# One feed-forward stage of a Flamingo kernel: the operations of a step in another order, with four slots for the picked rows

## The chip, the cores and the metric

The kernel runs on one core of a Trainium2 chip. A core has TensorE (PE in the profile; its weight loads are a row of their own, PEld), VectorE (DVE), ScalarE (ACT), GpSimd (POOL) and SyncE (SP, which here issues DMAs). Each engine works through its own instructions in the order in which they are written and is held only by semaphores. The metric is the device time of one execution in microseconds (us); less is better.

## The reference, cut to what matters

The program is eight residual blocks over x, 32 batches of 128 rows by 128 columns. The change is in the sixth, the controller feed-forward. A low-rank product gives 8 groups of 64 logits per row; in each group the first of the largest logits picks one hidden unit of 64, and only the picked units go through the second matrix.

```python
def _L2_ffn_ref(x, m1, m2, mb, w1, w2, b2):
    lr = xf @ m1
    mask_logits = jnp.einsum('bl,lxy->bxy', lr, m2) + mb
    quant_mask = jnp.argmax(mask_logits, axis=-1)
    ...
    w = w1p[j, quant_mask]
    mid = jnp.einsum('ai,aji->aj', xf, w)
    relu = jax.nn.relu(mid)
    v = w2p[j, quant_mask]
    res = jnp.einsum('ai,aij->aj', relu, v) + b2
...
x = x + jnp.tanh(g_ffn[2]) * _L2_ffn_ref(_layernorm(x, axis=-1), ...)
```

## The kernel before

The stage takes the 32 batches one after the other. x stays on chip. For one batch (128 rows on the partitions) the kernel computes all 512 hidden units and zeroes those that are not picked. The work of a batch, by engine, with the lines of the kernel before:

- ACT: normalises the rows (`xn`, L2031), copies the transposed rows out of PSUM (`xt`, L2039), copies the low-rank values (`low`, L2046), applies the relu to all hidden units (`full`, L2050), copies the transposed picked rows (`rt`, L2054).
- PE: transposes `xn` (L2117), multiplies by m1 (L2130, "low"), by m2 (L2113, "logits"), by w1 (L2127), transposes the picked rows in four pieces (L2135, "picked transposes"), multiplies them by w2 (L2123, "y").
- DVE, with the names used below: **top** (L2078, largest logit of each group, out of PSUM), **compare** (L2085, logit >= top, written to `pick`), then on GpSimd **count** (L2018, `pick` times a descending count, so that of equal logits the first has the largest value), then on DVE again **code** (L2074, the largest count of each group), **first** (L2081, count == code), **product** (L2091, that mask times the relu of the w1 row, written to `pick`), at last **update** (L2095, adds gate times y to x) and **statistics** (L2098, `bn_stats` of the new rows for the next block's layernorm).
- GpSimd also adds the bias row to x (L2014).

Top, compare, code, first and product each work on 128x512 numbers. `pick` has two slots, one per batch in turn.

The order is written out by hand: each engine has a function `step` that lists what it does in one step for different batches, and `pipeline4` calls it. In step b of the kernel before, DVE does code of batch b-1, top of b, first of b-1, compare of b, product of b-1, update of b-2 and statistics of b-2. `pipeline4` writes out steps -1 to 3, loops over steps 4 to 29, two to a turn of the loop, and writes out the last four. Semaphores (`ge_ready` from compare, `coded` from count, `picked_ready` from product, and so on) hold an engine until its operand is there, or until a buffer is free. Another stage of the same program, `attention_over_heads`, already runs four steps to a turn of its loop; it is `pipeline6` in the kernel before.

## Time and profile before

| | us |
|---|---|
| median of 3 runs (1623.01 to 1623.5) | 1623.44 |
| the profiled execution | 1622.37 |
| its span in the trace | 1620.6 |
| PE busy in the span | 1384.5 |
| DVE busy in the span | 1004.6 |
| POOL busy in the span | 769.8 |
| ACT busy in the span | 734.3 |

The profiled execution lasted 1.77 us longer than its span, and 1.07 us less than the median of the runs. The shares of the whole span mix eight blocks with different limits, so the stage that is changed has to be looked at by itself: it runs from about 816 to 965 us of the span.

### The profile page before, as it was taken

The page shows a single profiled execution, that of the slowest core. Times are in us where ns is not written, and L with a number is a line of the kernel's source. Part 1 is how long each engine was busy: PE and PEld are TensorE (multiplying, and loading weights), DVE is VectorE, ACT ScalarE, POOL GpSimd, SP SyncE. Part 2 cuts the span into 40 slices and gives each one's busy share as a digit, 9 for nine tenths or more (in the row PEclk, how much of TensorE's full clock was granted, in tenths as well). Part 3 has the DMA queues.
Part 4 walks back from the last instruction along what each step waited for, and adds up shares of the span by engine and source line. Part 5 has one row for each costly group of instructions (what it writes and reads, how often), then busy time and mean ns, then how long its engine had stood idle before and what let it go on. Part 6 is the DMA issues. An engine that isn't in the chain of part 4 may idle for free. (4 is left out here: it accounts for less than half of the span.)

```text
span 1620.6 us, 33970 instructions
## 1 busy us (share of the span) xinstructions
PE 1384.5 (85%) x10919; PEld 1114.7 (69%) x10919; DVE 1004.6 (62%) x2272; ACT 734.3 (45%) x1831; POOL 769.8 (47%) x989
## 2 busy tenths in 40 slices
PE   4998776989756786999978977999999999696996
PEld 3777556989756564777745546887788777486984
DVE  4887862413388486999868873555656755363555
ACT  3677453323366544666544443445554454221121
POOL 2554582345272363555635433544444677206445
PEclk9999897999955796999989998999999999798999
DMA  6500033759210000000000000000000000375942
GB/s 187 191 1 2 13 106 90 214 167 270 83 43 10 1 1 1 1 0 0 2 0 0 0 1 0 1 0 0 1 2 1 11 21 15 107 228 171 300 144 85
DMA packets 96490, 100.08 MB, mean 62 GB/s; under 512 B 12149, under 2 KB 69677, under 8 KB 95726
## 3 DMA queue, kind: packets, MB, share of 16 engines
q1 hardware_dynamic: 62322, 69.60, 14.2%
q0 software_dynamic: 8192, 16.79, 3.5%
q10 hardware_dynamic: 25852, 12.09, 2.7%
q8 instruction: 70, 1.15, 0.3%
q14 instruction: 54, 0.44, 0.1%
HBM read 72.23 MB, written 26.21 MB: 61 GB/s over the span
## 5 line engine op out<-in xcount | busy, mean ns | idle before, releaser
L2229 POOL TENSOR_TENSOR exp_scores_xattn<-exp_scores_xattn,softmax_recip_xattn 128x1640 f32<-128x1640 f32 x32 | 93.5, 2922 | 162.6 <-DVE softmax_recip_xattn L2402 162.6
L1469 PE MATMUL psum<-sorted_transposed_ffn,tile_weights_up_ffn 128*128 128x128 f32 x1280 | 164.8, 283 | 4.2 <-DVE sorted_transposed_ffn L1357 4.1
L1469 PEld LDWEIGHTS psum<-sorted_transposed_ffn,tile_weights_up_ffn 128*128 128x128 f32 x1280 | 154.2, 197 | 11.5 <-DVE sorted_transposed_ffn L1357 11.3
L1243 POOL DMA_INDIRECT gathered_rows_ffn<-sorted_y,slot_ffn x96 | 90.7, 945 | 105.2 <-DMA sorted_y<-expert_rows_ffn 46.8
L798 POOL TENSOR_TENSOR exp_scores<-exp_scores,softmax_recip 128x308 f32<-128x308 f32 x128 | 97.5, 784 | 78.9 <-DVE softmax_sum L892 78.9
L1479 PE MATMUL psum<-expert_weights_down_ffn,hidden_ffn 128*128 x960 | 123.8, 280 | 3.4 <-issue 2.8
L445 POOL TENSOR_TENSOR exp_scores<-exp_scores,softmax_recip 128x308 f32<-128x308 f32 x128 | 85.8, 702 | 80.1 <-DVE softmax_recip L614 79.9
L1232 POOL DMA_INDIRECT sorted_x<-xn_ffn,slot_ffn x64 | 61.3, 958 | 131.3 <-DVE slot_ffn L1117 112.3
L1479 PEld LDWEIGHTS psum<-expert_weights_down_ffn,hidden_ffn 128*128 128x128 f32 x960 | 115.8, 195 | 5.5 <-issue 5.5
L2278 ACT ACTIVATE exp_scores_xattn<-psum,scaled_negated_max_xattn 128x205 f32<-128x205 f32 x256 | 106.6, 451 | 0.0
L2469 PE MATMUL psum<-kv_transposed_xattn,queries_xattn 128*128 128x205 f32 x512 | 97.8, 346 | 3.4 <-DVE queries_xattn L2407 3.4
L640 PE MATMUL psum<-identity,exp_scores 128*77 128x128 f32 x512 | 81.4, 287 | 20.9 <-POOL exp_scores L445 13.8
L1272 ACT ACTIVATE hidden_ffn<-psum 128x512 f32<-128x512 f32 x80 | 47.7, 597 | 110.9 <-PE psum L1469 110.9
L2256 ACT COPY kv_transposed_xattn<-psum 128x205 f32<-128x205 f32 x32 | 10.6, 332 | 191.5 <-PE psum L2482 191.5
L2469 PEld LDWEIGHTS psum<-kv_transposed_xattn,queries_xattn 128*128 128x128 f32 x512 | 90.8, 196 | 4.0 <-DVE queries_xattn L2407 3.9
L2018 POOL TENSOR_TENSOR pick_ffn<-pick_ffn,descending_count 128x512 f32<-128x512 f32 x32 | 52.4, 1637 | 73.7 <-DVE pick_ffn L2085 73.7
L640 PEld LDWEIGHTS psum<-identity,exp_scores 128*77 128x77 f32 x512 | 62.6, 155 | 30.7 <-issue 22.7
L932 PE MATMUL psum<-identity,exp_scores 128*77 128x128 f32 x512 | 80.3, 281 | 3.1 <-POOL exp_scores L798 1.1
L2349 DVE TENSOR_REDUCE negated_max_xattn<-psum 128x4 f32<-128x820 f32 x64 | 64.7, 1010 | 25.4 <-PE psum L2469 25.0
L1278 ACT ACTIVATE silu_ffn<-psum 128x512 f32<-128x512 f32 x40 | 23.9, 597 | 123.3 <-PE psum L1469 120.7
L1357 DVE COPY sorted_transposed_ffn<-psum 128x256 f32<-128x256 f32 x80 | 33.7, 422 | 73.6 <-PE psum L1447 73.5
L1387 DVE COPY expert_rows_ffn<-psum 128x256 f32<-128x256 f32 x80 | 33.9, 424 | 70.8 <-PE psum L1479 67.1
(391 smaller groups left out, 3671.2 us busy)
## 6 DMA issues: line engine op xcount, KB each, us to landing
tile_weights_up_ffn<-in_L_ffn_packed_dram SPq DMA_DIRECT2D x160, 256.0 KB, 3.2
sorted_rows_ffn<-sorted_x SPq DMA_DIRECT2D x80, 128.0 KB, 3.1
sorted_y<-expert_rows_ffn ACTq DMA_DIRECT2D x80, 128.0 KB
sorted_x<-zeros SPq DMA_DIRECT2D x4, 1280.0 KB, 13.2
x_residual<-in_x_dram SPq DMA_DIRECT2D x4, 512.0 KB, 11.3
expert_weights_down_ffn<-in_L_ffn_packed_dram SPq DMA_DIRECT2D x8, 256.0 KB, 15.1
sorted_x<-xn_ffn,slot_ffn POOLq DMA_INDIRECT x128, 2.3
gathered_rows_ffn<-sorted_y,slot_ffn POOLq DMA_INDIRECT x128, 2.8
```

Of the source, the lines that this page charges most:

```text
L445: nc.gpsimd.tensor_tensor(e[:, par, heads, :], e[:, par, heads, :], rec.to_broadcast([S, HG, KC]), ALU.mult).then_inc(s["probs_ready"], 1)
L640: last = nc.tensor.transpose(m.psum[0:KC, 4 + g % 2, h * S:(h + 1) * S], e[:, nxt, g * HG + h, :], m.ident[:, :])
L798: nc.gpsimd.tensor_tensor(ev, ev, recip[:, ring % 2, :].unsqueeze(1).to_broadcast([S, HG, KC]), ALU.mult).then_inc(s["probs_ready"], 1)
L932: last = nc.tensor.transpose(m.psum[0:KC, 4 + g % 2, h * S:(h + 1) * S], e[:, (ring - 2) % RING, g * HG + h, :], m.ident[:, :])
L1232: nc.gpsimd.indirect_dma_start(m.sorted_x[half][:, :], bass.IndirectOffsetOnAxis(slot[:, half, k, b:b + 1], 0), xn[:, half * HBATCH + b, : ...
L1243: nc.gpsimd.indirect_dma_start(yg[:, n % 4, k, :], None, m.sorted_y[half][:, :], bass.IndirectOffsetOnAxis(slot[:, half, k, b:b + 1], 0)). ...
L1469: mm = nc.tensor.matmul(m.psum[:, 2 * (n % 2) + half, to:to + SUB], w[:, n % DEPTH, u, at:at + 128], xst[:, n % 2, u * SUB:(u + 1) * SUB], ...
L1479: mm = nc.tensor.matmul(m.psum[:, 4 + n % 2, u * D:(u + 1) * D], hid[:, n % 2, c, u * 128:(u + 1) * 128], columns(n, u, c * D), start=(c = ...
L2229: nc.gpsimd.tensor_tensor(ev, ev, recip[:, par, :].unsqueeze(2).to_broadcast([S, H3, KV]), ALU.mult).then_inc(s["probs_ready"], 1)
L2278: ins = nc.scalar.activation(e[:, par, h, :], m.psum[:, h // HB, (h % HB) * KV:(h % HB + 1) * KV], ACT.Exp, scale=SCALE, bias=shift_bias[: ...
L2349: nc.vector.tensor_reduce(negmax[:, par, heads].rearrange("p (n h) -> p n h", h=HB), sv, AX.X, ALU.max, negate=True).then_inc(s["negmax_re ...
L2469: mm = nc.tensor.matmul(m.psum[:, h // HB, (h % HB) * KV:(h % HB + 1) * KV], q[:, par, h, :], kvt[:, par, :], start=True, stop=True)
```

## The change

The stage gets `pipeline_fours`, which is `pipeline6` of the attention stage under a new name and with the first and the last step as arguments; `has(b, lag)` says for a written-out step whether the batch b - lag exists. The attention stage's own order stays as it was. In the controller feed-forward

- the steps run from -3 to 34 (before: -1 to 33), steps 4 to 27 in a loop of four steps to a turn;
- `pick` has four slots in place of two;
- on DVE a step is now: compare of batch b, update of b-3, statistics of b-4, top of b+1, then code, first and product of b-1 in a row. From compare to product of one batch there are eight operations on DVE in place of five;
- on ACT the copy of the picked transposes stands ahead of the copy of `xt`, and the relu is the first of a step;
- on PE a step is: w1 of b+1, picked transposes of b-2, transpose of b+3, logits of b+2, y of b-2, low of b+3;
- on GpSimd count stands ahead of the bias, which runs three batches ahead.

What is computed is the same, with the same instructions on the same shapes. The core of the diff, with removed lines left out (they are in the functions above):

```diff
@@ -737,14 +737,19 @@
-def pipeline6(eng, step, n=B):
-    for b in range(-2, 4):
+def has(b, lag):
+    return not isinstance(b, int) or 0 <= b - lag < B
+def pipeline_fours(eng, step, first, end, n=B):
+    for b in range(first, 4):
         step(b, b % 4)
     with eng.Fori(0, (n - 8) // 4) as i:
         for u in range(4):
             step(i * 4 + 4 + u, u)
-    for b in range(n - 4, n + 3):
+    for b in range(n - 4, end):
         step(b, b % 4)
...
@@ -1987,6 +1988,7 @@
     gate = m.gate[:, 6:7]
     HID = MX * MY
     CH = HID // 128
+    RING = 4
     with ExitStack() as ctx:
         def sb(name, shape, dtype=F32):
             return ctx.enter_context(nc.sbuf_tensor(f"{name}_ffn2", shape, dtype))
@@ -1998,7 +2000,7 @@
         full = sb("all_hidden", [S, 2, HID])
         top = sb("top_logit", [S, MX])
         code = sb("pick_code", [S, MX])
-        pick = sb("pick", [S, 2, MX, MY])
+        pick = sb("pick", [S, RING, MX, MY])
         rt = sb("picked_transposed", [128, CH * S])
         with nc.Block() as block:
             @block.gpsimd
@@ -2008,53 +2010,52 @@
                 pool.wait_ge(s["ones_ready"], 1)
                 pool.wait_ge(s["row_ready"], 1)
...
+                def step(b, ring):
+                    if has(b, 0):
                         wait(pool, s["ge_ready"], b + 1)
...
+                        pv = pick[:, ring, :, :]
                         nc.gpsimd.tensor_tensor(pv, pv, m.down[:, 0:MY].unsqueeze(1).to_broadcast([S, MX, MY]),
                                                 ALU.mult).then_inc(s["coded"], 1)
-                pipeline4(pool, step)
+                    if has(b, -3):
+                        wait(pool, s["xn_ready"], b + 4)
+                        nc.gpsimd.tensor_tensor(m.x[:, b + 3, :], m.x[:, b + 3, :], row_b2[:, :], ALU.add).then_inc(s["bias_added"], 1)
+                pipeline_fours(pool, step, -3, B + 3)
             @block.scalar
             def _(act):
                 act.wait_ge(s["var_ready"], 1)
                 nc.scalar.activation(m.sd[:, :], m.var[:, :], ACT.Sqrt, bias=m.eps[:, 0:1]).then_inc(s["sd_ready"], 1)
                 act.wait_ge(s["shift_ready"], 1)
                 def normalise(b, slot):
                     nc.scalar.activation(xn[:, slot, :], m.x[:, b, :], ACT.Identity, scale=m.rstd[:, bass.ds(b, 1)],
                                          bias=m.shift[:, bass.ds(b, 1)]).then_inc(s["xn_ready"], 1)
...
+                def step(b, ring):
+                    par, nxt = ring % 2, 1 - ring % 2
+                    if has(b, 0):
                         wait(act, s["full_in_psum"], b + 1)
                         wait(act, s["picked_ready"], b - 1)
                         nc.scalar.activation(full[:, par, :], m.psum[:, 3 + par, :], ACT.Relu).then_inc(s["full_ready"], 1)
...
+                    if has(b, -2):
+                        wait(act, s["low_in_psum"], b + 3)
+                        wait(act, s["logits_in_psum"], b + 1)
+                        nc.scalar.copy(low[0:ML, par, :], m.psum[0:ML, 0, S:2 * S]).then_inc(s["low_ready"], 1)
+                    if has(b, 2):
+                        wait(act, s["rt_in_psum"], b - 1)
+                        wait(act, s["y_done"], b - 2)
                         nc.scalar.copy(rt[:, :], m.psum[:, 5, :]).then_inc(s["rt_ready"], 1)
+                    if has(b, -3):
+                        wait(act, s["xt_in_psum"], b + 4)
+                        wait(act, s["full_in_psum"], b + 2)
+                        nc.scalar.copy(xt[:, nxt, :], m.psum[:, 0, 0:S]).then_inc(s["xt_ready"], 1)
+                    if has(b, -4):
+                        wait(act, s["xt_in_psum"], b + 3)
+                        normalise(b + 4, par)
                 normalise(0, 0)
-                pipeline4(act, step)
+                pipeline_fours(act, step, -3, B + 3)
                 preload(nc, m, ACT.Sqrt)
             @block.vector
@@ -2065,78 +2066,83 @@
                 nc.vector.tensor_scalar(row_b2[:, :], row_b2[:, :], gate, None, ALU.mult).then_inc(s["row_ready"], 1)
                 wide = [S, MX, MY]
...
+                def statistics(b):
+                    wait(dve, s["x_done"], b + 1)
+                    nc.vector.bn_stats(m.moments[:, b, :], m.x[:, b, :])
+                def logits_of(slot):
+                    return m.psum[:, 1 + slot, :].rearrange("p (x y) -> p x y", y=MY)
+                def step(b, ring):
+                    par, nxt = ring % 2, 1 - ring % 2
+                    last = pick[:, (ring - 1) % RING, :, :]
+                    if has(b, 0):
+                        wait(dve, s["top_ready"], b + 1)
+                        wait(dve, s["rt_in_psum"], b - 3)
+                        nc.vector.tensor_tensor(pick[:, ring, :, :], logits_of(par), top[:, :].unsqueeze(2).to_broadcast(wide),
+                                                ALU.is_ge).then_inc(s["ge_ready"], 1)
+                    if has(b, 3):
+                        wait(dve, s["y_done"], b - 2)
+                        wait(dve, s["bias_added"], b - 2)
+                        nc.vector.scalar_tensor_tensor(m.x[:, b - 3, :], m.psum[:, 6, 0:D], gate, m.x[:, b - 3, :],
+                                                       ALU.mult, ALU.add).then_inc(s["x_done"], 1)
+                    if has(b, 4):
+                        statistics(b - 4)
+                    if has(b, -1):
+                        wait(dve, s["logits_in_psum"], b + 2)
+                        wait(dve, s["ge_ready"], b + 1)
+                        nc.vector.tensor_reduce(top[:, :], logits_of(nxt), AX.X, ALU.max).then_inc(s["top_ready"], 1)
+                    if has(b, 1):
                         wait(dve, s["coded"], b)
...
+                        wait(dve, s["first_ready"], b - 1)
+                        nc.vector.tensor_reduce(code[:, :], last, AX.X, ALU.max).then_inc(s["code_ready"], 1)
                         wait(dve, s["code_ready"], b)
...
+                        nc.vector.tensor_tensor(last, last, code[:, :].unsqueeze(2).to_broadcast(wide), ALU.is_equal).then_inc(s["first_ready"], 1)
                         wait(dve, s["first_ready"], b)
                         wait(dve, s["full_ready"], b)
...
-                pipeline4(dve, step)
+                        picked = last.rearrange("p x y -> p (x y)")
+                        nc.vector.tensor_tensor(picked, picked, full[:, nxt, :], ALU.mult).then_inc(s["picked_ready"], 1)
+                pipeline_fours(dve, step, -3, B + 3)
+                statistics(B - 1)
             @block.tensor
             def _(pe):
                 pe.wait_ge(m.later_loaded, m.later_count)
                 pe.wait_ge(s["ones_ready"], 1)
...
+                def step(b, ring):
+                    par, nxt = ring % 2, 1 - ring % 2
+                    if has(b, -1):
+                        wait(pe, s["xt_ready"], b + 2)
+                        wait(pe, s["full_ready"], b)
+                        nc.tensor.matmul(m.psum[:, 3 + nxt, :], xt[:, nxt, :], w1[:, :], start=True, stop=True).then_inc(s["full_in_psum"], 1)
+                    if has(b, 2):
+                        wait(pe, s["picked_ready"], b - 1)
+                        wait(pe, s["rt_ready"], b - 2)
+                        for c in range(CH):
+                            mm = nc.tensor.transpose(m.psum[:, 5, c * S:(c + 1) * S],
+                                                     pick[:, (ring - 2) % RING, :, :].rearrange("p x y -> p (x y)")[:, c * 128:(c + 1) * 128], m.ident[:, :])
+                        mm.then_inc(s["rt_in_psum"], 1)
+                    if has(b, -3):
+                        wait(pe, s["xn_ready"], b + 4)
+                        wait(pe, s["low_ready"], b + 3)
+                        nc.tensor.transpose(m.psum[:, 0, 0:S], xn[:, nxt, :], m.ident[:, :]).then_inc(s["xt_in_psum"], 1)
+                    if has(b, -2):
+                        wait(pe, s["low_ready"], b + 3)
+                        wait(pe, s["ge_ready"], b + 1)
                         nc.tensor.matmul(m.psum[:, 1 + par, :], low[:, par, :], m2[:, :], start=True, stop=True).then_inc(s["logits_in_psum"], 1)
...
+                    if has(b, 2):
                         wait(pe, s["rt_ready"], b - 1)
                         wait(pe, s["x_done"], b - 2)
                         for c in range(CH):
                             mm = nc.tensor.matmul(m.psum[:, 6, 0:D], rt[:, c * S:(c + 1) * S], w2[:, c, :], start=(c == 0), stop=(c == CH - 1))
                         mm.then_inc(s["y_done"], 1)
...
+                    if has(b, -3):
+                        wait(pe, s["xt_ready"], b + 4)
                         nc.tensor.matmul(m.psum[0:ML, 0, S:2 * S], m1[:, :], xt[:, nxt, :], start=True, stop=True).then_inc(s["low_in_psum"], 1)
...
-                pipeline4(pe, step)
+                pipeline_fours(pe, step, -3, B + 3)
 def latent_attention(nc, m, sem, r, clear):
```

**DVE, one step inside the loop, before.** `pick_ffn` is the slot of picked rows, `top_logit_ffn` the largest logits, `pick_code_ffn` the code, `all_hidden_ffn` the relu of the w1 row.

```order
L2074 TENSOR_REDUCE pick_code_ffn<-pick_ffn 128x8
L54 REGISTER_ALU
L2078 TENSOR_REDUCE top_logit_ffn<-psum 128x8
L2081 TENSOR_TENSOR pick_ffn<-pick_ffn,pick_code_ffn 128x512
L2085 TENSOR_TENSOR pick_ffn<-psum,top_logit_ffn 128x512
L2091 TENSOR_TENSOR pick_ffn<-pick_ffn,all_hidden_ffn 128x512
L2095 ISA
L2095 SCALAR_TENSOR_TENSOR x_residual<-psum,tanh_gates,x_residual 128x128
L2098 ISA
L2098 BN_STATS x_moments<-x_residual 128x6
```

**DVE, one step inside the loop, now.**

```order
L2082 TENSOR_TENSOR pick_ffn<-psum,top_logit_ffn 128x512
L2087 ISA
L2087 SCALAR_TENSOR_TENSOR x_residual<-psum,tanh_gates,x_residual 128x128
L2071 ISA
L2071 BN_STATS x_moments<-x_residual 128x6
L54 REGISTER_ALU
L2094 TENSOR_REDUCE top_logit_ffn<-psum 128x8
L2098 TENSOR_REDUCE pick_code_ffn<-pick_ffn 128x8
L2100 TENSOR_TENSOR pick_ffn<-pick_ffn,pick_code_ffn 128x512
L2104 TENSOR_TENSOR pick_ffn<-pick_ffn,all_hidden_ffn 128x512
```

Before, the code of a batch came three instructions behind its compare (product, update, statistics lie between), and code, first and product had one other instruction between each two. Now a batch's code comes a whole step behind its compare, and code, first and product follow one another directly; statistics no longer follows the update of its own batch.

**PE, one step inside the loop, before.** `L_w` stands for w1 and w2, `L_m_and_mb` for m2 with its bias, `L_m` for m1.

```order
L2113 MATMUL psum<-L_m_and_mb,low_rank_ffn 128x512
L54 REGISTER_ALU
L2117 MATMUL psum<-identity,xn_ffn 128x128
L2123 MATMUL psum<-L_w,picked_transposed_ffn 128x128 x4
L2127 MATMUL psum<-L_w,xt_ffn 128x512
L2130 MATMUL psum<-xt_ffn,L_m 64x128
L2135 MATMUL psum<-identity,pick_ffn 128x128 x4
```

**PE, one step inside the loop, now.**

```order
L2119 MATMUL psum<-L_w,xt_ffn 128x512
L2124 MATMUL psum<-identity,pick_ffn 128x128 x4
L54 REGISTER_ALU
L2130 MATMUL psum<-identity,xn_ffn 128x128
L2134 MATMUL psum<-L_m_and_mb,low_rank_ffn 128x512
L2139 MATMUL psum<-L_w,picked_transposed_ffn 128x128 x4
L2143 MATMUL psum<-xt_ffn,L_m 64x128
```

The picked transposes (L2135, now L2124) stood last in a step, right ahead of the next step's logits; now the w1 product stands ahead of them. They are also of batch b-2 in place of b-1.

## Rows read from the trace of the kernel before

**Rows 1.** Busy time by stretch: PE, PEld, DVE, ACT, POOL, then granted clock, DMA.

```profile
823.50:965.00 141.50, 124.45 (x603) 71.38 (x602) 116.75 (x225) 63.30 (x156) 64.81 (x62) 0.97 0.00 0
827.00:830.40 3.40, 3.40 (x7) 0.87 (x5) 2.49 (x4) 0.66 (x2) 0.53 (x1) 0.50 0.00 0
958.00:964.60 6.60, 3.63 (x24) 2.77 (x24) 3.86 (x10) 1.27 (x3) 1.21 (x1) 1.00 0.01 1
```

**Rows 2.** Timeline of DVE: start, length, engine, line, operation, tiles [idle before].

```profile
884.46 0.68 DVE L2085 TENSOR_TENSOR pick_ffn<-psum,top_logit_ffn 128x512 f32<-128x512 f32 x1
...
885.66 0.34 DVE L2095 SCALAR_TENSOR_TENSOR x_residual<-psum,tanh_gates,x_residual 128x128 f32 x1
886.14 0.29 DVE L2098 BATCH_NORM_STATS2 x_moments<-x_residual  x1
886.91 0.69 DVE L2074 TENSOR_REDUCE pick_code_ffn<-pick_ffn 128x8 f32<-128x512 f32 x1 [0.47 <-POOL pick_ffn L2018]
...
888.71 0.68 DVE L2085 TENSOR_TENSOR pick_ffn<-psum,top_logit_ffn 128x512 f32<-128x512 f32 x1
```

**Rows 3.** Timeline of POOL in the fill, and in the same step as rows 2.

```profile
824.44 1.26 POOL L2018 TENSOR_TENSOR pick_ffn<-pick_ffn,descending_count 128x512 f32<-128x512 f32 x1 [3.77 <-DVE pick_ffn L2085]
...
885.22 1.65 POOL L2018 TENSOR_TENSOR pick_ffn<-pick_ffn,descending_count 128x512 f32<-128x512 f32 x1 [2.20 <-DVE pick_ffn L2085]
```

**Rows 4.** Timeline of PE in the loop.

```profile
884.06 1.02 PE L2127 MATMUL psum<-L_w,xt_ffn 128*128 128x512 f32 x2
885.01 0.43 PE L2130 MATMUL psum<-xt_ffn,L_m 128*64 128x128 f32 x2
885.80 0.66 PE L2135 MATMUL psum<-identity,pick_ffn 128*128 128x128 f32 x4 [0.35 <-DVE pick_ffn L2091]
886.29 1.02 PE L2113 MATMUL psum<-L_m_and_mb,low_rank_ffn 65*128 65x512 f32 x2
887.15 0.27 PE L2117 MATMUL psum<-identity,xn_ffn 128*128 128x128 f32 x1
887.26 1.05 PE L2123 MATMUL psum<-L_w,picked_transposed_ffn 128*128 128x128 f32 x8
888.15 1.02 PE L2127 MATMUL psum<-L_w,xt_ffn 128*128 128x512 f32 x2
```

**Rows 5.** Timeline of DVE, the last steps of the stage.

```profile
959.24 0.69 DVE L2074 TENSOR_REDUCE pick_code_ffn<-pick_ffn 128x8 f32<-128x512 f32 x1 [0.57 <-POOL pick_ffn L2018]
959.96 0.69 DVE L2081 TENSOR_TENSOR pick_ffn<-pick_ffn,pick_code_ffn 128x512 f32<-128x512 f32 x1
960.68 0.69 DVE L2091 TENSOR_TENSOR pick_ffn<-pick_ffn,all_hidden_ffn 128x512 f32<-128x512 f32 x1
...
964.35 0.29 DVE L2098 BATCH_NORM_STATS2 x_moments<-x_residual 128x6 f32<-128x128 f32 x1
```

**Rows 6.** Timeline of DVE in the attention stage's loop, four steps to a turn.

```profile
660.05 0.34 DVE L916 SCALAR_TENSOR_TENSOR x_residual<-psum,tanh_gates,x_residual 128x128 f32 x1
660.35 0.80 DVE L886 TENSOR_TENSOR head_sums<-exp_scores 128x616 f32<-128x616 f32 x1
...
666.28 0.80 DVE L886 TENSOR_TENSOR head_sums<-exp_scores 128x616 f32<-128x616 f32 x1 [0.25 <-issue]
```

**Rows 7.** Timeline of PE, then of DVE, in the fill.

```profile
820.84 2.07 PE L2113 MATMUL psum<-L_m_and_mb,low_rank_ffn 65*128 65x512 f32 x2 [0.35 <-ACT low_rank_ffn L2046]
822.70 0.42 PE L2117 MATMUL psum<-identity,xn_ffn 128*128 128x128 f32 x1
822.92 1.91 PE L2127 MATMUL psum<-L_w,xt_ffn 128*128 128x512 f32 x2
824.76 0.69 PE L2130 MATMUL psum<-xt_ffn,L_m 128*64 128x128 f32 x2
...
829.71 0.68 DVE L2091 TENSOR_TENSOR pick_ffn<-pick_ffn,all_hidden_ffn 128x512 f32<-128x512 f32 x1
```

**Rows 8.** The product's 32 lengths: shortest, median, longest, first and last start.

```profile
L2091 DVE TENSOR_TENSOR pick_ffn<-pick_ffn,all_hidden_ffn x32: 678/680/693, 829.7 to 960.7; 128x512 f32<-128x512 f32 x32
```

More of the change, by code:

```diff
@@ L765, in attention_over_heads @@
     RING = 4
-    def has(b, lag):
-        return not isinstance(b, int) or 0 <= b - lag < B
     with ExitStack() as ctx:
@@ L810, in step @@
                         scale(ring, range(1, NG))
-                pipeline6(pool, step)
+                pipeline_fours(pool, step, -2, B + 3)
             @block.scalar
@@ L991, in step @@
                         transposes(b, ring, 3)
-                pipeline6(pe, step)
+                pipeline_fours(pe, step, -2, B + 3)
 class Routing:
@@ L2032, in normalise @@
                                          bias=m.shift[:, bass.ds(b, 1)]).then_inc(s["xn_ready"], 1)
-                def step(b, par, front, middle, back, tail):
-                    nxt = 1 - par
-                    if front:
-                        wait(act, s["xt_in_psum"], b + 2)
-                        wait(act, s["full_in_psum"], b)
-                        nc.scalar.copy(xt[:, nxt, :], m.psum[:, 0, 0:S]).then_inc(s["xt_ready"], 1)
-                    if front and not (isinstance(b, int) and b + 2 >= B):
-                        wait(act, s["xt_in_psum"], b + 1)
-                        normalise(b + 2, par)
-                    if front:
-                        wait(act, s["low_in_psum"], b + 2)
-                        wait(act, s["logits_in_psum"], b)
-                        nc.scalar.copy(low[0:ML, nxt, :], m.psum[0:ML, 0, S:2 * S]).then_inc(s["low_ready"], 1)
-                    if middle:
+                def step(b, ring):
+                    par, nxt = ring % 2, 1 - ring % 2
+                    if has(b, 0):
                         wait(act, s["full_in_psum"], b + 1)
@@ L2066, in _ @@
                 wide = [S, MX, MY]
-                def step(b, par, front, middle, back, tail):
-                    nxt = 1 - par
-                    pv = pick[:, nxt, :, :]
-                    if back:
-                        wait(dve, s["coded"], b)
-                        nc.vector.tensor_reduce(code[:, :], pv, AX.X, ALU.max).then_inc(s["code_ready"], 1)
-                    if middle:
-                        wait(dve, s["logits_in_psum"], b + 1)
-                        logits = m.psum[:, 1 + par, :].rearrange("p (x y) -> p x y", y=MY)
-                        nc.vector.tensor_reduce(top[:, :], logits, AX.X, ALU.max).then_inc(s["top_ready"], 1)
-                    if back:
-                        wait(dve, s["code_ready"], b)
-                        nc.vector.tensor_tensor(pv, pv, code[:, :].unsqueeze(2).to_broadcast(wide), ALU.is_equal).then_inc(s["first_ready"], 1)
-                    if middle:
-                        wait(dve, s["top_ready"], b + 1)
-                        wait(dve, s["rt_in_psum"], b - 1)
-                        nc.vector.tensor_tensor(pick[:, par, :, :], logits, top[:, :].unsqueeze(2).to_broadcast(wide),
-                                                ALU.is_ge).then_inc(s["ge_ready"], 1)
-                    if back:
@@ L2105, in _ @@
                 pe.wait_ge(s["ones_ready"], 1)
-                def step(b, par, front, middle, back, tail):
-                    nxt = 1 - par
-                    if middle:
-                        wait(pe, s["low_ready"], b + 1)
-                        wait(pe, s["ge_ready"], b - 1)
-                        nc.tensor.matmul(m.psum[:, 1 + par, :], low[:, par, :], m2[:, :], start=True, stop=True).then_inc(s["logits_in_psum"], 1)
-                    if front:
-                        wait(pe, s["xn_ready"], b + 2)
-                        wait(pe, s["low_ready"], b + 1)
-                        nc.tensor.transpose(m.psum[:, 0, 0:S], xn[:, nxt, :], m.ident[:, :]).then_inc(s["xt_in_psum"], 1)
-                    if tail:
+                def step(b, ring):
[18 more added lines that the diff above has]
+                        wait(pe, s["ge_ready"], b + 1)
+                        nc.tensor.matmul(m.psum[:, 1 + par, :], low[:, par, :], m2[:, :], start=True, stop=True).then_inc(s["logits_in_psum"], 1)
+                    if has(b, 2):
                         wait(pe, s["rt_ready"], b - 1)
```

34 lines of the change are left out of this document (2 added, 32 removed).

## The prediction, made before the changed kernel was run

> **What bounds the stage now.** I read the busy time by stretch first. In the 141.5 us of the stage PE is busy for 124.5 us and DVE for 116.8 us [rows 1]: neither is full, and no transfer runs, so something goes round between engines. The timeline of DVE over one step shows what. From one compare to the next it is 888.71 - 884.46 = 4.25 us, and in each step DVE stands idle once, for 0.47 us ahead of code, until POOL's count has ended [rows 2]. The timeline of POOL closes the ring: compare starts at 884.46, count at 885.22 (0.76 later), code at 886.91 (1.69 later), and behind code stand top, first and the next compare, three starts in 1.80 us [rows 2, 3]. 0.76 + 1.69 + 1.80 = 4.25: the whole period. The reader is to see that compare of batch b waits behind first of b-1, which waits for count of b-1. DVE's own work would take 0.47 us less. PE follows: it waits 0.35 us in the shown step for the product [rows 4].
>
> **What the change does to this ring.** Count of batch b starts when compare has ended, 0.76 us into DVE's step, and is done at 2.45; code of b is now in the next step, and nothing of DVE's own step waits for count. The slack is some 3 us (code starts about 1.7 us into the next step, 3.7 + 1.7 - 2.45). So the 0.47 us goes. The four slots carry this: a slot is written again four batches later, so compare need not wait for the picked transposes of its own slot (they end within two steps). More slots add no instruction; with only two, compare of b would have to wait for the transposes of b-2, which PE does in the same step.
>
> **What a DVE step costs now.** The sum of the start-to-start times in the new order:
>
> - compare to update 0.60, the pitch of independent wide operations (1.80 for three) [rows 2].
> - update to statistics 0.30: statistics is now of the batch before and waits for nothing in front of it. An update followed by an operation independent of it is 0.30 long [rows 6]; in the stage's loop, dependent, it was 0.48 [rows 2].
> - statistics to top 0.20: it is 0.29 long [rows 2], and DVE's operations start about 0.08 ahead of their predecessor's end (0.68 long, 0.60 apart) [rows 2].
> - top to code 0.60.
> - code to first, first to product 0.72 each. These pairs are now neighbours, each reading what the one in front wrote. The last batch of the stage before shows exactly this pair: 959.24, 959.96, 960.68 [rows 5]. That is 0.12 more than independent neighbours, twice a step.
> - product to the next compare 0.60.
>
> Sum 3.74 us, against 4.25: the stall and the statistics' dependence go, two dependent pairs come. Below, the pairs cost 0.60 each: 3.50. Above, update to statistics stays at 0.48 and statistics holds top to its end and a little more (0.33): 4.05. I take 3.74, because rows 5 are these very instructions and rows 6 come from a loop of this very form. Such a loop also costs something at each return: 0.25 us of idle that nothing releases, and the start that is no longer early, 0.28 together [rows 6], once per four steps, six times.
>
> The Trainium skill (VectorE: DVE Perf Modes, section "The DRAIN you can't avoid") says that a chain of operations with a semaphore after each takes no longer than one without. By that rule first and product would cost no more than any neighbour, the sum would be 3.50, and the stage some 7.4 us shorter than by mine. Rows 5 against rows 2 differ by 0.12 for the same shapes, so I go by the rows.
>
> **What is late next.** PE's own step, from starts in the loop: w1 0.95, low at most its length 0.43, picked transposes 0.49, logits 0.86, transpose 0.11, y 0.89 [rows 4]: 3.73 at most, 3.52 if low costs as much as two of y's eight pieces (0.22). So PE is nearly as full as DVE and close behind it, but not ahead. Its waits: the relu of b now stands first on ACT and waits for product of b-2 (two slots of `full`); the copy of low is queued behind it, and transpose and logits wait for that copy. From the product's end this is relu 0.59, copy 0.26 and the two hand-overs, about 0.9 us, while PE is in the picked transposes for 0.5 to 0.6 of it. PE then trails DVE by some 0.3 us a step, but its delay doesn't come back: top of b+1 uses logits that PE made a step earlier, update uses y of a step earlier. ACT's copy of the picked transposes ahead of `xt` comes in time for y, which has logits (0.86) in front of it. GpSimd's bias, three batches ahead, has the rest of count's step.
>
> **The sum.** From the first product to the last it was 960.68 - 829.71 = 130.97 us [rows 5, 7], 31 steps. Now: 27 full steps of 3.74 are 100.98; step 2 has neither update nor statistics and its top stands right behind compare (0.72 + 0.60 + 0.72 + 0.72 + 0.60 = 3.36); step 3 lacks statistics (3.54); step 31 has no top (3.14); step 32 neither top nor compare (2.54). With six loop returns of 0.28 this is 115.2: **15.7 us less**.
>
> Against this stands the fill. The first product now stands behind top of batch 2, so PE must have made three logits before it. At half clock (0.50 until 830.4) [rows 1] logits take 1.86, a transpose 0.22, w1 1.84, and low between 0.44 (twice 0.22) and its length of 0.69 [rows 7]. A round is 4.4 to 4.6. The first logits started at 820.84; they now have a transpose in front of them, 821.06, so the third start at 829.8 to 830.3 and, with the clock rising on the way, end at about 831.4. Top, code, first: 0.1 + 0.60 + 0.72 + 0.72 put the first product at 833.5, **3.8 us later** than before. Bounds 3.4 and 4.4 (clock rising a microsecond earlier or later). The tail behind the last product is the same chain as before, with one more statistics at the end: 0.2 us.
>
> Net 15.7 - 3.8 - 0.2 = 11.7. I round to 11.5. The profiled execution was 1622.37, so 1610.9; the median of the runs lies 1.07 above it, at 1623.44. **Forecast for the median: 1612.0 us.** The later stages start earlier and are otherwise as they were; no transfer ran in the stage that could now come too late [rows 1].
>
> **The rivals.**
>
> 1. *A step costs more than 3.74.* The order adds semaphore and register work to DVE's short operations, or PE at 3.73 plus its own loop return is the bound. At 4.05 over 27 steps 8.4 us of the gain go: 1620.3. For it: PE's sum is within 0.01 of DVE's at its upper bound. Against it: rows 6. Chance 0.20 for 1615.5 to 1620.2.
> 2. *Dependent neighbours cost nothing* (the skill's rule above). DVE's step is 3.50 and PE's 3.52 is the bound: 27 steps of 0.22 and the short ones give some 7 us more, 1605. Against it: rows 5. Chance 0.07, under 1609.
> 3. *Nothing gained: POOL and DVE slow each other.* Count took 1.26 us with DVE idle and 1.65 beside DVE [rows 3]. If in the new overlap DVE's operations were stretched by the same 0.39 a step, 31 steps lose 12.1 us: 1624. Against it: product ran beside count in every step and its length hardly moved, 678 to 693 ns [rows 8]. The Trainium skill (GPSIMD Engine Reference, section "Key points") has GpSimd contend with VectorE instructions that have two SBUF inputs; here the rows show the loss on POOL's side, where there is slack. Chance 0.08 for no change.
> 4. *Slower: PE's clock stays at its lower level.* In the fill it is 0.50, the lower level [rows 1]. A PE step there costs twice 3.52, or 3.3 us more than DVE's step. The gain of 11.5 is used up after 3.5 such steps, and 4.5 make the kernel measurably slower; a rise 35 us later (9 steps) gives 1642. For it: the fill is rearranged. Against it: with 0.50 until 830.4 the whole stretch still has 0.97, so the clock rose there and stayed, after a fill as nearly unbroken as the new one; and it was 1.00 in the stage's tail with PE busy for 3.63 of 6.60 us [rows 1]. Chance 0.05.
>
> **Numbers.** Forecast as it stands (1609 to 1615.5) 0.60. The range 1606 to 1619 takes in most of rivals 1 and 2, and leaves out about 0.2. A measurement of this kernel can tell about 0.2%, 3.2 us, from no change: under 1620.2 is faster, 0.60 + 0.20 + 0.07 = 0.87; same 0.08; slower 0.05.
>
> **What would show it.** Right: no idle ahead of code (L2098 in the new kernel) put down to count; compares 3.7 to 3.8 us apart, with one longer gap in four; first 0.72 behind code, and product 0.72 behind first; the first product near 833.5 and the last near 949. Wrong: idle on DVE ahead of top or update released by PE (rival 1), wide DVE operations above 0.69 (rival 3), or a granted clock under 1.00 past 840 us (rival 4).

## The result, and the profile after

| | before | changed |
|---|---|---|
| median of the runs, us | 1623.22 (4 runs, 1622.12 to 1623.5) | 1610.57 (4 runs, 1607.57 to 1612.35) |
| ratio to before | | 0.9927 (95%: 0.9913 to 0.9941) |
| span of the profiled execution, us | 1620.6 | 1605.8 |
| the stage in that span, us | 148.57 | 134.66 |

The kernel is faster by 0.73%, 11.9 us (9.6 to 14.1); the medians of the table alone lie 12.65 us apart, inside that range. The stage is taken here and below from the first operation of its layernorm (`x_mean_doubled` on DVE) to the same operation of the next block:

```profile
813.69 0.22 DVE L317 TENSOR_TENSOR x_mean_doubled<-x_moments 128x32 f32<-128x32 f32 x1 [0.55 <-PEq L790]
...
948.35 0.22 DVE L317 TENSOR_TENSOR x_mean_doubled<-x_moments 128x32 f32<-128x32 f32 x1 [0.31 <-PEq L2005]
```

Before, these two stood at 816.37 and 964.94. The stage gave 13.9 us of the 14.8 us between the two spans. What lies ahead of it was 2.7 us shorter in this execution and what lies behind it 1.8 us longer, with the same code: that much moves by itself from run to run, so small effects are read from the stage, and the smallest from the step, since PE's clock moves the stage's two ends too (shown with the experiments).

Busy time over 95 us of the steady steps (PE, PEld, DVE, ACT, POOL, then granted clock and DMA), to be held against [rows 1]:

```profile
840.00:935.00 95.00, 95.00 (x486) 60.07 (x485) 93.22 (x180) 48.90 (x125) 43.01 (x51) 1.00 0.00 0
```

PE has no idle time left and DVE 1.8 us in 95. One step of DVE, from compare to compare, which answers to [rows 2]:

```profile
879.58 0.68 DVE L2082 TENSOR_TENSOR pick_ffn<-psum,top_logit_ffn 128x512 f32<-128x512 f32 x1
880.18 0.34 DVE L2087 SCALAR_TENSOR_TENSOR x_residual<-psum,tanh_gates,x_residual 128x128 f32 x1
880.44 0.28 DVE L2071 BATCH_NORM_STATS2 x_moments<-x_residual  x1
880.64 0.67 DVE L2094 TENSOR_REDUCE top_logit_ffn<-psum 128x8 f32<-128x512 f32 x1
881.23 0.68 DVE L2098 TENSOR_REDUCE pick_code_ffn<-pick_ffn 128x8 f32<-128x512 f32 x1
881.94 0.69 DVE L2100 TENSOR_TENSOR pick_ffn<-pick_ffn,pick_code_ffn 128x512 f32<-128x512 f32 x1
882.66 0.69 DVE L2104 TENSOR_TENSOR pick_ffn<-pick_ffn,all_hidden_ffn 128x512 f32<-128x512 f32 x1
883.27 0.68 DVE L2082 TENSOR_TENSOR pick_ffn<-psum,top_logit_ffn 128x512 f32<-128x512 f32 x1
```

The wait ahead of code is gone and a step is 3.69 us. Code to first is 0.71 and first to product 0.72, where independent neighbours stand 0.59 to 0.61 apart. POOL in the same step, beside [rows 3]:

```profile
880.34 1.27 POOL L2017 TENSOR_TENSOR pick_ffn<-pick_ffn,descending_count 128x512 f32<-128x512 f32 x1 [2.02 <-DVE pick_ffn L2082]
881.57 0.46 POOL L2021 TENSOR_TENSOR x_residual<-x_residual,L_b_row 128x128 f32 x1
```

Count is 1.27 us long in place of 1.65. It ends at 881.61, the bias behind it at 882.03, and first starts at 881.94. One step of PE, beside [rows 4]:

```profile
877.36 0.60 PE L2124 MATMUL psum<-identity,pick_ffn 128*128 128x128 f32 x4
877.80 0.27 PE L2130 MATMUL psum<-identity,xn_ffn 128*128 128x128 f32 x1
877.91 1.02 PE L2134 MATMUL psum<-L_m_and_mb,low_rank_ffn 65*128 65x512 f32 x2
878.77 1.05 PE L2139 MATMUL psum<-L_w,picked_transposed_ffn 128*128 128x128 f32 x8
879.76 0.43 PE L2143 MATMUL psum<-xt_ffn,L_m 128*64 128x128 f32 x2
880.12 1.13 PE L2119 MATMUL psum<-L_w,xt_ffn 128*128 128x512 f32 x2
881.08 0.60 PE L2124 MATMUL psum<-identity,pick_ffn 128*128 128x128 f32 x4
```

PE takes 3.72 us in this step, 3.73 in the mean of the loop, and waits for nothing: the two engines are nearly even, with PE 0.03 to 0.04 us a step behind.

### The profile page after: what moved, and what is told of

It is laid out like the page before. It is cut to its first block and busy times, and to the rows that moved or that the text cites. A ratio compares the mean times of both kernels' runs of the same rounds, so it can differ in the third digit from the quotient of the medians.

```text
span 1605.8 us, 33990 instructions
## 1 busy us (share of the span) xinstructions
PE 1376.9 (86%) x10919; PEld 1113.0 (69%) x10919; DVE 1004.9 (63%) x2272; ACT 732.2 (46%) x1831; POOL 757.8 (47%) x989
## 5 line engine op out<-in xcount | busy, mean ns | idle before, releaser
L2524 PE MATMUL psum<-probs_t_context_xattn,kv_kept_xattn 77*128 77x512 f32 x128 | 68.0, 612 | 9.2 <-ACT probs_t_latents_xattn L2276 8.4
## 6 DMA issues: line engine op xcount, KB each, us to landing
x_residual<-in_x_dram SPq DMA_DIRECT2D x4, 512.0 KB, 10.9
```

The lines of the kernel that those rows point to most:

```text
L2524: nc.tensor.matmul(m.psum[:, 4 + half, :], kept[0:KC, nxt, 0, :], ptc[:, cols], start=True, stop=False)
```

## The experiments

All times are in us. The stage is that of one profiled execution. "Step" is the mean distance between DVE's compares from batch 8 to batch 24, from the timeline; PE's granted clock is 1.00 there in every kernel.

| kernel | median | before, same chip | ratio (95%) | stage | step |
|---|---|---|---|---|---|
| before | 1623.22 | | | 148.57 | 4.26 |
| changed | 1610.57 | 1623.22 | 0.9927 (0.9913 to 0.9941) | 134.66 | 3.70 |
| before_half_count | 1619.8 | 1622.14 | 0.9979 (0.9964 to 0.9993) | 145.58 | 4.18 |
| before_late_transposes | 1625.32 | 1622.66 | 1.0016 (1.0004 to 1.0029) | 151.01 | 4.25 |
| before_half_count_late_transposes | 1611.41 | 1622.66 | 0.995 (0.9933 to 0.9967) | 136.34 | 3.79 |
| after_two_slots | 1644.36 | 1622.14 | 1.0131 (1.0104 to 1.0158) | 169.31 | 4.76 |
| after_rt_copy_last | 1626.93 | 1622.14 | 1.0031 (1.0019 to 1.0044) | 151.30 | 4.35 |
| after_count_twice | 1639.68 | 1622.14 | 1.0098 (1.0073 to 1.0124) | 165.42 | 4.71 |
| after_interleaved | 1616.68 | 1622.66 | 0.9966 (0.9951 to 0.9981) | 140.13 | 3.89 |
| after_interleaved_clear_of_count | 1609.17 | 1622.66 | 0.9923 (0.9902 to 0.9944) | 133.05 | 3.73 |
| after_three_pieces | 1608.84 | 1620.88 | 0.9923 (0.9904 to 0.9942) | 134.36 | 3.69 |
| clear_of_count_three_pieces | 1602.28 | 1620.88 | 0.9886 (0.9862 to 0.9909) | 125.02 | 3.45 |
| clear_of_count_early_pe | 1607.82 | 1620.88 | 0.9911 (0.9895 to 0.9928) | 133.05 | 3.74 |

A stage also holds what PE's clock did at its two ends, and that is not the edits' doing alone. The changed kernel and after_three_pieces (below) have the same PE instructions in the fill, and their first transposes start at 816.33 and 816.40. These rows, one of each kernel, show the stretch in which the granted clock rises from 0.50 to 1.00 (last column but two):

```profile
828.00:829.00 1.00, 1.00 (x3) 0.10 (x2) 0.00 (x0) 0.97 (x3) 0.44 (x1) 0.84 0.00 0
```

```profile
824.00:826.00 2.00, 2.00 (x6) 0.63 (x5) 0.96 (x2) 0.76 (x3) 0.46 (x1) 0.81 0.00 0
```

So it rose 12.0 us after the first transpose in one and 8.4 in the other, and the first product came 17.36 and 15.67 us after the stage's start. In before it rose after 11.9 us; over all kernels, after 8.4 to 15.5. In the last 7 to 11 us of the stage the clock fell to 0.50 again in before_late_transposes, after_two_slots, after_count_twice, after_interleaved and after_three_pieces, and stayed at 1.00 in the others. Differences between stages of some 2 us are therefore not read by themselves; the step is.

### Was count's ring the bound of before?

The first kernel makes count shorter in the order of before.

```diff
-                        pv = pick[:, par, :, :]
-                        nc.gpsimd.tensor_tensor(pv, pv, m.down[:, 0:MY].unsqueeze(1).to_broadcast([S, MX, MY]),
+                        pv = pick[:, par, 0:MX // 2, :]
+                        nc.gpsimd.tensor_tensor(pv, pv, m.down[:, 0:MY].unsqueeze(1).to_broadcast([S, MX // 2, MY]),
```

Expected: 

> The order of before, with count on 4 of the 8 groups, about 0.85 us in place of 1.65 (leaves out half of the count). Theory (the ring compare, count, code, top, first sets before's step of 4.25 us): the ring falls to some 3.45 us, DVE's own 3.78 us or PE's 3.75 us takes over, so 0.45 us x 31 steps: 12 to 14 us less than before, as much as the whole change. Rival (PE's order makes the gain, POOL's wait is only where PE's limit shows): 0 to 2 us less.

The stage fell by 3.0 us, not by 12 to 14, and the step from 4.26 to 4.18. The theory of one ring, as the prediction had it, failed here. DVE's and PE's timelines of this kernel show what took over:

```profile
883.65 0.69 DVE L2074 TENSOR_REDUCE pick_code_ffn<-pick_ffn 128x8 f32<-128x512 f32 x1
884.64 0.69 DVE L2078 TENSOR_REDUCE top_logit_ffn<-psum 128x8 f32<-128x512 f32 x1 [0.30 <-PE psum L2113]
...
886.44 0.68 DVE L2091 TENSOR_TENSOR pick_ffn<-pick_ffn,all_hidden_ffn 128x512 f32<-128x512 f32 x1
...
887.18 0.66 PE L2135 MATMUL psum<-identity,pick_ffn 128*128 128x128 f32 x4 [0.35 <-DVE pick_ffn L2091]
887.75 1.12 PE L2113 MATMUL psum<-L_m_and_mb,low_rank_ffn 65*128 65x512 f32 x2
...
888.90 0.69 DVE L2078 TENSOR_REDUCE top_logit_ffn<-psum 128x8 f32<-128x512 f32 x1 [0.29 <-PE psum L2113]
```

Code no longer waits, but top does, for PE. From top to product it is 1.80, to the picked transposes 0.74, to the logits queued behind them 0.57, to the next top 1.15: 4.26 us (4.10 in the other step of the loop's turn). So before had a second ring, product, transposes, logits, top, just under the first. The next two kernels cut it by PE's order, with the full count and with half of it.

```diff
 PE, one step:
-  logits(b), transpose(b+1), y(b-2), w1(b), low(b+1), picked transposes(b-1)
+  logits(b), picked transposes(b-2), transpose(b+1), w1(b), low(b+1), y(b-2)
 ACT, one step:
-  xt(b+1), normalise(b+2), low(b+1), relu(b), rt(b-1)
+  rt(b-2), xt(b+1), normalise(b+2), low(b+1), relu(b)
```

Expected: 

> The order of before on DVE and POOL, full count; on PE the picked transposes of b-2 behind the logits of b, and y last, ACT's copy of them first. Theory of two rings (one over count, 4.25 us; one over product, picked transposes, logits, top, 4.1 to 4.25): this cuts only the second, the first stays: within 2 us of before. Rival (PE's order alone is the gain): 10 us under before.

Expected: 

> The same with count on 4 of 8 groups (leaves out half of the count). Theory of two rings: both are cut, DVE's own 3.78 us a step is left, 0.45 us x 31: 12 to 14 us under before, though each of the two edits alone gives 0 to 3. Rival (a third wait holds the step at 4.1 or more): under 4 us.

With the full count the step stayed at 4.25, and the stage got 2.4 us longer at its two ends, where the clock rose later (15.5 us after PE's first transpose) and fell to 0.50 before the end. With half of the count the step fell to 3.79 and the stage by 12.2 us, as expected; the whole kernel, by its ratio, by 8.1 (5.4 to 10.9). Alone the two edits take 0.08 and 0.01 us off the step, together 0.47: two rings of nearly the same length, and the gain comes only when both are cut. The changed kernel cuts both, since it makes the logits two batches ahead and transposes the picked rows two steps behind.

### The other parts of the change

Two slots in place of four:

```diff
-    RING = 4
+    RING = 2
...
-                        wait(dve, s["rt_in_psum"], b - 3)
+                        wait(dve, s["rt_in_psum"], b - 1)
```

Expected: 

> The changed kernel with two slots of picked rows in place of four, so that compare of b waits for the picked transposes of b-2, which PE does in the same step. Theory: DVE stands 0.6 to 0.75 us a step ahead of compare, steps of 4.35 to 4.45 us, 20 to 24 us above the changed kernel, some 10 us above before. Rival (the transposes end in time, slots are no part of the gain): the changed kernel's time.

The stage is 34.7 us longer than the changed kernel's, more than the expected 20 to 24. DVE's timeline:

```profile
885.09 0.69 DVE L2104 TENSOR_TENSOR pick_ffn<-pick_ffn,all_hidden_ffn 128x512 f32<-128x512 f32 x1
886.72 0.69 DVE L2082 TENSOR_TENSOR pick_ffn<-psum,top_logit_ffn 128x512 f32<-128x512 f32 x1 [0.94 <-PE psum L2124]
```

Compare waits 0.93 to 1.01 us a step in the loop (0.6 to 0.75 expected): the w1 product stands ahead of the transposes on PE and is still running when product ends. The slots are a condition of the gain.

ACT's copy of the picked transposes moved to the end of its step:

```diff
-                    if has(b, 2):
-                        wait(act, s["rt_in_psum"], b - 1)
-                        wait(act, s["y_done"], b - 2)
-                        nc.scalar.copy(rt[:, :], m.psum[:, 5, :]).then_inc(s["rt_ready"], 1)
                     if has(b, -3):
...
                         normalise(b + 4, par)
+                    if has(b, 2):
+                        wait(act, s["rt_in_psum"], b - 1)
+                        wait(act, s["y_done"], b - 2)
+                        nc.scalar.copy(rt[:, :], m.psum[:, 5, :]).then_inc(s["rt_ready"], 1)
```

Expected: 

> The changed kernel with ACT's copy of the picked transposes last in the step, behind the copy of xt and the normalise. Theory (PE is full at 3.73 us a step and y waits for this copy): the copy comes 0.6 to 0.7 us later, y too, and PE's step grows by as much: 16 to 20 us above the changed kernel, 4 to 8 us above before. Rival (DVE alone sets the step and PE's delay stays behind it): within 2 us of the changed kernel.

The stage grew by 16.6 us, as expected. PE waits for the copy, and DVE in turn for y:

```profile
883.74 1.16 PE L2139 MATMUL psum<-L_w,picked_transposed_ffn 128*128 128x128 f32 x8 [0.36 <-ACT picked_transposed_ffn L2055]
...
885.04 0.35 DVE L2087 SCALAR_TENSOR_TENSOR x_residual<-psum,tanh_gates,x_residual 128x128 f32 x1 [0.56 <-PE psum L2139]
```

So a delay on PE does come back to DVE, through update, as soon as PE's step is the longer one.

### Do POOL and DVE hold each other up?

Count done twice, on POOL:

```diff
...
+                        nc.gpsimd.tensor_tensor(pv, pv, down, ALU.mult).then_inc(s["counted_once"], 1)
+                        wait(pool, s["counted_once"], b + 1)
                         nc.gpsimd.tensor_tensor(pv, pv, down, ALU.mult).then_inc(s["coded"], 1)
```

Expected: 

> The changed kernel, with count done twice in a row on POOL (2.6 us or more in place of 1.27). Theory (count has some 3 us of slack now, DVE does not feel it): within 1.5 us of the changed kernel, 12 us under before. Rival (POOL and DVE slow each other where DVE reads two operands from SBUF): first and product get 0.2 us longer each in the steps, 10 to 12 us above the changed kernel, so about before's time.

My theory was wrong, and the rival too small: the stage is 30.8 us longer. DVE and POOL, from their timelines:

```profile
882.51 1.57 DVE L2102 TENSOR_TENSOR pick_ffn<-pick_ffn,pick_code_ffn 128x512 f32<-128x512 f32 x1
884.11 0.83 DVE L2106 TENSOR_TENSOR pick_ffn<-pick_ffn,all_hidden_ffn 128x512 f32<-128x512 f32 x1
...
882.26 1.27 POOL L2020 TENSOR_TENSOR pick_ffn<-pick_ffn,descending_count 128x512 f32<-128x512 f32 x1
883.48 0.91 POOL L2023 TENSOR_TENSOR x_residual<-x_residual,L_b_row 128x128 f32 x1
```

First (here L2102) is issued while the second count runs and is 1.57 us long, 0.88 more than alone. It ends at 884.08, 0.55 after that count; the bias, issued while first is there, is 0.91 in place of 0.46 and ends 0.31 after first; product is held by the rest of the bias (0.83). They do not share, they take turns. All of these read two tensors from SBUF. Statistics, top and code read one there at most; they start at 881.01, 881.21 and 881.80, beside the first count (880.91 to 882.18), and keep their lengths of 0.28, 0.67 and 0.67.

Whether this decides the order of DVE's step, the next two kernels show. Both put something between the dependent neighbours; the first places first beside count, the second behind it.

```diff
 DVE, one step:
-  changed:         compare(b), update(b-3), statistics(b-4), top(b+1), code(b-1), first(b-1), product(b-1)
+  interleaved:     compare(b), code(b-1), update(b-3), first(b-1), statistics(b-4), top(b+1), product(b-1)
+  clear of count:  compare(b), code(b-1), top(b+1), statistics(b-4), first(b-1), update(b-3), product(b-1)
```

Expected: 

> The changed kernel with DVE's step as compare, code, update, first, statistics, top, product, so that no operation reads what its neighbour wrote. Theory (a DVE instruction with two SBUF operands and one of POOL's wait for each other): first starts 1.5 us into the step, while count runs from 0.76 to 2.03, and is held for some 0.55 us; steps of about 4.0 us, 7 to 11 us above the changed kernel. Rival (no such wait, only the dependent pairs cost): DVE at 3.46 us a step, PE at 3.73 is the bound, 1 to 3 us under the changed kernel.

Expected: 

> The changed kernel with DVE's step as compare, code, top, statistics, first, update, product: no dependent neighbours, and first starts at 2.0 us, when count ends. Theory: DVE's step falls to some 3.5 us, PE at 3.73 us becomes the bound, and only the tail is shorter: 0 to 3 us under the changed kernel. Rival (DVE sets the step, PE follows it): 5 to 7 us under the changed kernel. If first is held by the bias too: 0 to 5 us above.

The first, beside count, costs 5.5 us of stage (7 to 11 expected) and 0.19 us a step: 0.43 of turn, less 0.24 for the two dependent pairs that are gone. The second saves 1.6 us of stage. Their rows of first, one after the other, the second with what stands in front of it on DVE and POOL's bias:

```profile
882.87 1.12 DVE L2095 TENSOR_TENSOR pick_ffn<-pick_ffn,pick_code_ffn 128x512 f32<-128x512 f32 x1
```

```profile
883.33 0.69 DVE L2091 TENSOR_REDUCE top_logit_ffn<-psum 128x8 f32<-128x512 f32 x1 [0.16 <-PE psum L2136]
883.89 0.46 POOL L2021 TENSOR_TENSOR x_residual<-x_residual,L_b_row 128x128 f32 x1
...
884.14 0.75 DVE L2096 TENSOR_TENSOR pick_ffn<-pick_ffn,pick_code_ffn 128x512 f32<-128x512 f32 x1
```

Beside count, first is 1.12 us (0.43 of turn, 0.55 expected). Behind count it still meets the bias, which POOL starts at once: 0.75 here, 0.67 to 0.98 from step to step. And now top waits for PE's logits. In steps 4 to 7 the compares of this order stand 3.44 to 3.45 apart, later 3.73 in the mean, as PE's logits do: DVE has become the faster engine.

### Which engine binds the changed kernel?

One of y's four pieces left out, in the changed order and in the order clear of count:

```diff
-                        for c in range(CH):
-                            mm = nc.tensor.matmul(m.psum[:, 6, 0:D], rt[:, c * S:(c + 1) * S], w2[:, c, :], start=(c == 0), stop=(c == CH - 1))
+                        for c in range(CH - 1):
+                            mm = nc.tensor.matmul(m.psum[:, 6, 0:D], rt[:, c * S:(c + 1) * S], w2[:, c, :], start=(c == 0), stop=(c == CH - 2))
```

Expected: 

> The changed kernel with three of the four pieces of y (leaves out a quarter of the second matrix's product): PE's step falls from 3.73 to about 3.5 us, DVE's stays at 3.70. Theory (DVE and PE are even; PE alone made shorter leaves DVE): 0 to 3 us under the changed kernel. Rival (PE is the only bound): 6 us or more under it.

Expected: 

> The order clear of count, with three of four pieces of y: both DVE and PE near 3.5 us a step. Theory (each alone gives little, since the other takes over): 0.2 us x 27 steps, 5 to 8 us under the changed kernel. Rival (something else holds 3.7 us a step): under 3 us.

The step of the changed kernel is 3.70. A shorter PE alone leaves it at 3.69, the shorter DVE alone at 3.73, PE's own; both bring it to 3.45. Neither engine is the bound by itself; they are level at 3.7 us, and each hides what is taken from the other. The stages say the same (0.3, 1.6 and 9.6 us less; 5 to 8 expected for both), but with the clock in them: of the 9.6, 7.2 lie between the first and the last product and 2.3 in the fill, where the clock rose 8.5 us after the first transpose in place of 12.0.

### An earlier clock

```diff
                 pe.wait_ge(m.later_loaded, m.later_count)
+                for t in range(10):
+                    nc.tensor.transpose(m.psum[:, 7, 0:S], m.ident[:, :], m.ident[:, :])
                 pe.wait_ge(s["ones_ready"], 1)
```

Expected: 

> The order clear of count, and ten transposes of the identity into an unused bank on PE while it would wait for the first normalised rows, so that its clock may rise earlier. Theory (the clock rose some 12 us after PE's first work in the stage, work 2 to 3 us earlier moves the rise by as much, at half clock half of that is lost work): 1 to 1.5 us under the order clear of count, so 13 to 16 us under before. Rival (nothing moves, or the first transpose is held up): 0 to 1 us above it.

Nothing moved, as the rival had it: the stage is 133.05 us with and without. PE's timeline, then its clock around the ten transposes (columns as in [rows 1]):

```profile
815.96 1.39 PE L2115 MATMUL psum<-identity 128*128 128x128 f32 x10 [1.27 <-PEq L790]
818.55 0.47 PE L2134 MATMUL psum<-identity,xn_ffn 128*128 128x128 f32 x1 [1.20 <-POOL low_rank_ffn L2009]
...
829.84 1.43 PE L2138 MATMUL psum<-L_m_and_mb,low_rank_ffn 65*128 65x512 f32 x2
```

```profile
815.90:816.50 0.60, 0.54 (x5) 0.57 (x6) 0.51 (x4) 0.00 (x0) 0.00 (x0) 1.00 0.00 0
816.50:817.40 0.90, 0.85 (x7) 0.50 (x5) 0.48 (x3) 0.32 (x1) 0.00 (x0) 0.77 0.00 0
817.40:818.50 1.10, 0.00 (x0) 0.00 (x0) 0.71 (x3) 0.49 (x1) 0.30 (x1) 0.50 0.00 0
```

The ten transposes did not run at the lower clock: it was still 1.00, and fell to 0.50 while the last of them ran, near 817.0. PE then stood idle for 1.20 us, and the clock rose inside the third logits (1.43 long, between 1.92 and 1.02), 12.1 us after the stage's own first transpose, as in the changed kernel (12.0). So the theory, earlier work at the lower clock, was not put to the test; and with a rise that lies between 8.4 and 12.0 us after the same fill, one execution could not have settled it. By the runs neither this kernel (0.9911, 0.9895 to 0.9928) nor the order clear of count can be told from the changed kernel; their stages are 1.6 us shorter.

## Why the prediction was right, point by point

- **The sum** was 15.7 - 3.8 - 0.2 = 11.7 us for the stage; in the two profiled executions it is 18.0 - 4.0 - 0.1 = 13.9. The forecast of 1612.0 for the median measured 1610.57. The three terms are taken up below.
- **The ring over count** was there and is cut: no idle time ahead of code is left. But "DVE's own work would take 0.47 us less" took it for the only ring. The second one, product, picked transposes, logits, top, was 0.08 us a step shorter (4.18 against 4.26) and would have kept nearly all of the gain. The forecast held because the change cuts that one too. The prediction counted on what cuts it ("top of b+1 uses logits that PE made a step earlier"), but did not see that in before the wait for these logits stood right behind the wait for count. That both were cut was luck in this respect.
- **The step of 3.74 us** measured 3.69. The dependent pairs cost 0.71 and 0.72, as taken from [rows 5]; update to statistics is 0.26 (0.30). The Trainium skill (VectorE: DVE Perf Modes, "The DRAIN you can't avoid") has a semaphore between neighbours cost nothing, measured on eight copies; here each such pair costs 0.11 to 0.12 us more than an independent one. The order clear of count bears out the price: without these pairs and with a shorter PE the step is 3.45.
- **The loop's return** was priced at 0.28 from [rows 6] and cost DVE nothing: its compares stand 3.69 to 3.70 apart from step 4 to step 20, with no longer gap among them. This term, 1.7 us, was wrong.
- **PE at 3.73 at most** was right to 0.01, by errors that cancel: low takes 0.36 (0.43) and the picked transposes 0.44 (0.49), but y 0.99 (0.89). That its delay "doesn't come back" holds only while its step is no longer than DVE's. Here it is 0.03 to 0.04 longer, and from step 21 on the delay does come back: update stands up to 0.65 behind compare in place of 0.60, and the compares 3.71 to 3.75 apart. With 32 batches this is some 0.2 us.
- **The fill** was put 3.8 us later. From the stage's start to the first product it is 831.05 - 813.69 = 17.36, before 829.71 - 816.37 = 13.34 [rows 7]: 4.0 later. The forecast took the clock to rise when it did in before, and in this execution it did; in after_three_pieces, with the same fill, the first product came 1.7 us sooner. That part is luck. **The tail** is 0.1 us longer (948.35 - 944.02 against 964.94 - 960.68).
- **The products** span 944.02 - 831.05 = 112.97 us, 18.0 less than before, where 15.7 was forecast. The loop's return (1.7) and 0.04 us a step (1.1) make 2.8; three firsts that POOL held up, 0.82 to 0.89 long, take 0.5 back. These two rows are:

```profile
831.05 0.69 DVE L2104 TENSOR_TENSOR pick_ffn<-pick_ffn,all_hidden_ffn 128x512 f32<-128x512 f32 x1
...
944.02 0.69 DVE L2104 TENSOR_TENSOR pick_ffn<-pick_ffn,all_hidden_ffn 128x512 f32<-128x512 f32 x1
```

- **Rival 3 was dismissed on a wrong reading.** That product kept its length beside count [rows 8] was read as "the loss is on POOL's side, where there is slack". It kept its length because it was issued ahead of count; count waited for it (1.65 against 1.27). In the other sequence DVE waits. The Trainium skill (GPSIMD Engine Reference, "Key points") says that GpSimd contends with VectorE instructions that have two SBUF inputs, and the rows agree. The "slack of some 3 us" is count's slack for its result; for the turn there is almost none. Behind count POOL starts the bias at once, and in the rows above where first met an operation of POOL it ended 0.55 us after it (after_count_twice, after_interleaved). In the step shown the bias ends at 882.03, so first could have ended at 882.58; it ended at 882.63. By these 0.05 us the change stays clear of it in the steady steps, and the time came out as forecast; the prediction does not price this, so it is luck. In the fill it does not stay clear: first of batch 1 meets the bias and is 0.89 long.

```profile
833.77 0.89 DVE L2100 TENSOR_TENSOR pick_ffn<-pick_ffn,pick_code_ffn 128x512 f32<-128x512 f32 x1
...
833.65 0.45 POOL L2021 TENSOR_TENSOR x_residual<-x_residual,L_b_row 128x128 f32<-128x128 f32 x1
```

- **Rival 4** did not come: the granted clock is 1.00 in all of 840 to 935, and in this execution to the end of the stage. The tail of before was a weak argument against it: in five of the kernels above the clock fell to 0.50 in the tail, and in after_three_pieces the stretch behind the last product took 5.72 us in place of 4.33.

## What to carry to other kernels

When a wait is found on a ring between engines, follow every other operand of the ring's operations back by one period as well: a second ring of nearly the same length takes the place of the first when only that one is cut. When a step's order is changed, look not only at whether a result comes in time, but also at which two-operand operations of POOL and DVE will now run at the same time. Where two engines are level, shorten both or neither. And hold executions against each other in stretches with the same granted clock: a rise that came 3.6 us later, with the same instructions, went with 1.7 us here, more than some of the edits gave.

## What the runs showed of the hardware that was not expected

- A DVE operation with two SBUF tensors and a POOL operation of that kind take turns: the one that comes second waits. So an engine is held not only by semaphores, as the opening has it. Count beside product was 0.38 us longer with 512 columns (1.65 against 1.27) and again 0.38 with 256 (1.11 against 0.73, in before_half_count): a wait of fixed length, not a slower rate. First beside the second count reached 1.57 us in place of 0.69.
- A turn of a loop of four steps cost DVE nothing in this stage, while the attention stage's loop shows 0.25 us [rows 6]. The runs do not say why they differ.
- y's eight pieces take 0.99 us ahead of low, 0.99 ahead of the logits (before_late_transposes) and 0.89 ahead of w1, with the same instructions; the experiments do not say why.
- With the same instructions in front of it, PE's clock rose 8.4 us after the first transpose in one kernel and 12.0 in another. What decides between them is open.
